# A home of their own for a pair's rows, statistics two tiles ahead, and a later wait for the low-rank operands in a fused attention and FFN kernel

## The reference, cut to what matters

```python
xn = _layernorm(x)                        # x: (4, 512, 1024), over the last axis
qkv = xn @ w_qkv                          # 32 query heads, 8 key and 8 value heads of 128
scores = einsum('bqhgd,bkhd->bhgqk', q, k) * scale
bias = -slope[h] * sqrt(max(pos_q - pos_k, 0)), -inf where pos_k > pos_q
attn = einsum(softmax(scores + bias), v) @ w_o
out = xn @ W.T + b                        # the FFN branch, 1024 x 1024
probs = softmax(xn @ gate_w.T + gate_b)   # 4 experts; one chosen, weight top / top
out += (xn @ A[:r].T @ B[:, :r].T) of the chosen rank r in (8, 16, 32, 64)
x + attn + out
```

## Time and profile before

| | us |
|---|---|
| median of three runs | 2610.23 (2610.15 to 2610.34) |
| the profiled execution's own time | 2612.52 |
| its span, first to last instruction | 2610.7 |
| PE busy | 2495.8 (96% of the span) |
| DVE busy | 1639.0 (63%) |
| ACT busy | 1026.0 (39%) |
| POOL busy | 174.7 (7%) |
| mean granted TensorE clock | 0.982 |

### The profile page before, as it was taken

How to read it: one execution, slowest core, us unless ns; L and a number is a source line. 1 busy time by engine, 2 the same in 40 slices (tenths; PEclk the granted TensorE clock), 3 DMA queues, 4 the chain that set the end, 5 groups by cost and what they waited for, 6 DMA issues and landing times.

```text
span 2610.7 us, 32277 instructions
## 1 busy us (share of the span) xinstructions
PE 2495.8 (96%) x12512; PEld 2129.1 (82%) x12512; DVE 1639.0 (63%) x3305; ACT 1026.0 (39%) x2123; POOL 174.7 (7%) x230
## 2 busy tenths in 40 slices
PE   4999899997799989999799999999999999999998
PEld 3788688886678868888688888888888888888887
DVE  5746534564655545545767776777767776777763
ACT  4533212333534311333444444444444444444441
POOL 2210100001220010000100000000000000000000
PEclk8999999998999989999899999999999999999999
DMA  4545534555245453544632232323344232322321
GB/s 143 167 131 190 186 133 141 193 201 192 85 140 185 168 187 113 193 177 162 246 105 99 96 117 93 105 82 121 121 162 148 95 113 97 106 100 95 114 72 65
DMA packets 86489, 355.09 MB, mean 136 GB/s; under 512 B 8873, under 2 KB 9017, under 8 KB 77376
## 3 DMA queue, kind: packets, MB, share of 16 engines
q1 hardware_dynamic: 49680, 216.65, 24.1%
q0 software_dynamic: 36656, 136.38, 14.8%
HBM read 235.02 MB, written 117.97 MB: 135 GB/s over the span
## 4 chain that ended last, share of the span: by engine, by line
PE 91%; DVE 4%; issue 2%; ACT 2%; DMA 1%; POOL 0%; SPq 0%; DVEq 0%; ACTq 0%; POOLq 0%
PE ps L512 28%; PE ps L514 28%; PE ps L513 28%; PE ps L699 5%; PE ps L595 1%; DVE stats L968 1%; ACT res_hi L753 0%; DMA rows_a<-x 0%; DVE w_lo L953 0%; DVE res_a L1044 0%; DVE res_a L953 0%; DVE res_b L953 0%; DVE res_b L1044 0%; DMA qk_s<-res_b 0%; ACT w_hi L753 0%
## 5 line engine op out<-in xcount | busy, mean ns | idle before, releaser
L953 DVE TENSOR_TENSOR w_lo<-raw,w_hi 128x1024 fp32r<-128x1024 f32 x196 | 238.9, 1223 | 374.0 <-ACT w_hi L753 373.9
L512 PE MATMUL ps<-x_hi,w_hi 128*128 128x512 f32 x1120 | 436.2, 389 | 0.0
L514 PE MATMUL ps<-x_hi,w_lo 128*128 128x512 f32 x1120 | 435.8, 389 | 0.0
L513 PE MATMUL ps<-x_lo,w_hi 128*128 128x512 f32 x1120 | 435.7, 389 | 0.0
L753 ACT ACTIVATE w_hi<-raw 128x1024 fp32r<-128x1024 f32 x196 | 207.0, 1059 | 580.6 <-PE ps L514 458.8
L512 PE MATMUL ps<-wo_hi,at_hi 128*128 128x512 f32 x1024 | 411.6, 402 | 1.4 <-DVE at_lo L953 1.4
L514 PE MATMUL ps<-wo_hi,at_lo 128*128 128x512 f32 x1024 | 400.6, 391 | 0.0
L513 PE MATMUL ps<-wo_lo,at_hi 128*128 128x512 f32 x1024 | 398.2, 389 | 0.0
L892 ACT ACTIVATE probs<-probs,neg_max 128x512 f32<-128x512 f32 (+3 forms) x512 | 283.6, 563 | 193.6 <-DVE neg_max L1189 193.6
L1222 DVE TENSOR_TENSOR acc<-ps,acc 128x512 f32<-128x512 f32 x256 | 176.6, 690 | 164.2 <-issue 135.4
L753 ACT ACTIVATE at_hi<-ps 128x512 fp32r<-128x512 f32 x128 | 76.7, 599 | 509.9 <-PE ps L514 509.9
(11 more groups left out here) (151 smaller groups left out, 4062.4 us busy)
## 6 DMA issues: line engine op xcount, KB each, us to landing
raw<-w_all SPq DMA_DIRECT2D x70, 1024.0 KB, 5.1
q<-qk_s SPq DMA_DIRECT2D x128, 512.0 KB, 3.8
qk_s<-res_hi POOLq DMA_DIRECT2D x40, 1024.0 KB, 4.6
wo_raw<-w_o SPq DMA_DIRECT2D x64, 512.0 KB, 4.3
qk_s<-res_a POOLq DMA_DIRECT2D x20, 1024.0 KB, 9.0
qk_s<-res_b POOLq DMA_DIRECT2D x20, 1024.0 KB, 5.3
k<-qk_s SPq DMA_DIRECT2D x32, 512.0 KB, 3.8
v<-v_s SPq DMA_DIRECT2D x32, 512.0 KB, 5.8
```

The costliest lines, as they stand in the source:

```text
L512: pe.matmul(to, st_hi, mv_hi, start=start, stop=False, skip_group_check=True)
L513: pe.matmul(to, st_hi, mv_lo, start=False, stop=False, skip_group_check=True)
L514: return pe.matmul(to, st_lo, mv_hi, start=False, stop=stop, skip_group_check=True)
L953: nc.vector.tensor_tensor(to, source, high.bitcast(F32), ALU.subtract).then_inc(signal, 1)
```

## The change

- The eight rows of a pair get a buffer `rows` of 32 KB at offset 16 KB, which is the place of `x_hi` slots 2 to 5; tile t lies over slot t + 2. SP loads tile t of the second pair once LAST's step t + 2 has ended, its last reader. `rows_a`, `rows_b` and their reuse go. At the start of the program SP issues the four rows of tiles 0 and 1, then the first weights, the four rows of tiles 2 and 3, and the other three weight blocks.
- Statistics, reciprocals and normalisation of a tile go together and run two tiles ahead: tile 1 at st 5 of LAST, tile 2 at st 6, tile 3 after copies of turn 1 and `second_tile(0)`. At the start of the program tile 1 stands before the first weights, tile 2 behind them.
- Turns 2 and 3 wait for `s_x0_lo` (the low part copied out of the bank) where they waited for `s_t1`, since the order of the DVE no longer implies it.
- FFN goes from fourth to sixth of the matrices, right before LAST.
- PE waits for `s_lora_in` and `s_u_lo` right before the first `lora` product of step 1.

```diff
-VALUES, KEYS, Q0, FFN, Q1, Q2, Q3 = range(MATRICES)
+VALUES, KEYS, Q0, Q1, Q2, FFN, Q3 = range(MATRICES)
...
-        rows_a = at("rows_a", 192 * K, [P, 3, HIDDEN])
-        rows_b = at("rows_b", 168 * K, [P, 2, HIDDEN])
+
+        rows = at("rows", 16 * K, [P, TT, HIDDEN])
...
+            def tokens(pr, t):
+
+                if pr:
+                    sp.wait_ge(s_bank, 4 * (number(pr - 1, LAST, t + 2) + 1))
+                for j in range(2):
+                    sp.dma_start(rows[:, 2 * t + j, :],
...
-                if m == FFN and st == 1:
-                    pe.wait_ge(s_u_lo, 3 * (pr + 1))
-                    pe.wait_ge(s_lora_in, 32 * (pr + 1))
...
                         if kt == KT - 1 and extra is not None:
+                            if st == 1 and s == 0:
+                                pe.wait_ge(s_u_lo, 3 * (pr + 1))
+                                pe.wait_ge(s_lora_in, 32 * (pr + 1))
                             last = lora(bank_of(n, s), s, *extra)
...
                     if t >= 2:
-                        pe.wait_ge(s_t1, pr * QT + t)
+                        pe.wait_ge(s_x0_lo, pr * QT + t)
...
                 for t in range(1, QT):
                     turned_tile(pr, t)
-                    if t + 1 < QT:
-                        deviation(pr, t + 1)
                     second_tile(pr, t - 1)
-                    if t + 1 < QT:
-                        normalised(pr, t + 1)
+                    if t + 2 < QT:
+                        deviation(pr, t + 2)
+                        normalised(pr, t + 2)
...
                     if st == 5:
                         deviation(pr + 1, 1)
+                        reciprocals(pr + 1, 1)
                     if st == 6:
                         turned_tile(pr + 1, 0)
-                        reciprocals(pr + 1, 1)
+                        deviation(pr + 1, 2)
+                        reciprocals(pr + 1, 2)
```

More of the change, by code:

```diff
@@ L134, in block_program @@
         s_const = sem("s_const")
-        s_rows = [sem(f"s_rows{i}") for i in range(5)]
+        s_rows = [sem(f"s_rows{i}") for i in range(TT)]
         s_raw = [sem(f"s_raw{i}") for i in range(4)]
@@ L260, in loaded @@
             return 16 * ((2 * g + 2) if st == 6 else (2 * g + 1) if WEIGHT[st] == 3 else g + 1)
[L264 to L268, removed]
         def turned(pr, t):
@@ L309, in _ @@
             sp.dma_start(ident[:, :], consts[:, SEQ:SEQ + P]).then_inc(s_ident, 16)
[L311 to L320, removed]
+            def tokens(pr, t):
[3 more added lines that the diff above has]
+                    sp.dma_start(rows[:, 2 * t + j, :],
+                                 x[bass.ds((pr * 2 + j) * SEQ + t * P, P), :]).then_inc(s_rows[2 * t + j], 16)
             def weights(pr, m, i, st):
@@ L330, in _ @@
             weights(0, 0, 0, None)
-            for i in range(2, 5):
-                tokens(0, i)
+            tokens(0, 2)
+            tokens(0, 3)
             for i in range(1, 4):
                 weights(0, 0, i, None)
-            for i in range(5, TT):
-                tokens(0, i)
             for pr in range(PAIRS):
@@ L351, in _ @@
                     sp.dma_start(raw[3][:, :], w_all[m, 3]).then_inc(s_raw[3], 16)
+                    if m == LAST and follow is not None:
+                        tokens(pr + 1, 0)
                     if follow is not None:
@@ L362, in _ @@
                         if m == LAST:
-                            for i in range(5, TT):
-                                tokens(pr + 1, i)
+                            tokens(pr + 1, 3)
             sp.wait_ge(s_bank, 4 * (number(PAIRS - 1, LAST, 2) + 1))
@@ L780, in normalised @@
                 for j in range(2):
-                    tile = row_tile(pr, 2 * t + j)[0]
+                    tile = rows[:, 2 * t + j, :]
                     nc.scalar.activation(tile, tile, ACT.Identity, bias=shift[:, 2 * t + j:2 * t + j + 1],
@@ L964, in deviation @@
                 for j in range(2):
-                    tile, landed = row_tile(pr, 2 * t + j)
-                    dve.wait_ge(*landed)
+                    dve.wait_ge(s_rows[2 * t + j], 16 * (pr + 1))
                     for half in range(2):
-                        last = nc.vector.bn_stats(stats[:, j, half, :], tile[:, half * 512:(half + 1) * 512])
+                        last = nc.vector.bn_stats(stats[:, j, half, :],
+                                                  rows[:, 2 * t + j, half * 512:(half + 1) * 512])
                 link(last)
```

39 lines of the change are left out of this document (21 added, 18 removed).

## The result

| | before | after |
|---|---|---|
| median of the runs on the same chip, us | 2610.19 (2608.99 to 2610.34) | 2571.05 (2568.85 to 2574.92) |
| profiled execution's time / span, us | 2612.52 / 2610.7 | 2568.85 / 2567.1 |
| PE busy | 2495.8 | 2485.7 |
| mean granted TensorE clock | 0.982 | 0.991 |

The ratio of the medians is 0.9853, with an interval of 0.9836 to 0.987. The time is 39.1 us less by the medians and 43.6 by the two profiled spans. The two differ because of the executions that were profiled: before, it lay 2.3 us above its median, and now it is the fastest of its four. In the runs further down the kernel before lies anywhere from 2608.2 to 2613.82 us, so two of its executions agree within 0.2%, not within a few hundredths. Two of its executions in the second group of experiments were slow runs (5045.9 and 5865.81 us) and are left out of all that follows.

The account below looks back on a forecast made before the run. PE's waits were taken to bound the kernel, at both first steps and in FFN. Gains of 8.1 + 9.3 + 23.0 = 40.4 us off 2610.2 gave 2569.8 us, range 2562 to 2580.

Parts of the forecast that it names:

- What bounds the kernel: PE's waits count in three places: both first steps, chains through DVE, ACT and PE, and FFN.
- Start of pair 0: At program start, turn 3 comes at 42.8 and step 1 at 53.7, 8.1 us earlier; bounds 5 and 14.
- Between the pairs: Turn 0 gains 3.5 us, turn 1 2.0, and step 1 comes 9.3 us earlier; bounds 2.0 and 14.
- FFN: Step 1's later wait for low-rank operands gains 11.2 and 11.8 us, together 23.0; ends 20 and 24.9.
- I charge no clock: In FFN's step 1, matmuls behind the remaining waits of 1.3 and 1.1 us run without a slow clock.
- Sum and median: Whole kernel: gains sum to 40.4 us, span 2570.3, median of runs 2569.8.
- Small DVE operations behind POOL: Rival, first steps: POOL's operations hold reciprocals, 1.0 us more each, up to 9 in all: 2577; chance 0.10.
- PE's pace: Rival: the loops run at PE's pace and both first steps gain 14 us: 2559; chance 0.07.
- Operands later: Rival in FFN: low-rank operands land 3 us later each: 2576; chance 0.06.
- nothing in the first steps: Rival: a wait as long takes its place in the first steps, only 23.0 gained: 2587; chance 0.05.
- The clock stays low: Rival: after first-step waits the clock stays at 1.2 GHz, 0.2 us more per matmul, some 2620 after 250; chance 0.04.
- FFN sixth costs nothing: Moving FFN to sixth, with rows at 16 KB, adds no instruction and was costed at nothing.

Follow-up runs that it names:

- old_order: Changed kernel with statistics back in their old order (one tile ahead, weights ahead of turn 0's copies), rows in the new buffer: 2577.63 us.
- adds_first: Changed kernel, but in LAST's step 6 of pair 0 DVE does step 5's adds before the next matrix's first low half: 2568.49 us.
- after_again: The changed kernel run again without edit, as base on the chip of a later group: 2577.26 us.
- copies_first: adds_first, with ACT also copying LAST's step 6 into `res_hi` before tile 2's square root and normalisation: 2565.6 us.
- start_too: copies_first, with tile 2's statistics at program start ahead of the first weights' low halves, its square root between their high halves: 2559.99 us.
- late_only: The kernel before with only the wait for the low-rank operands moved late: 2591.23 us.
- ffn_fourth: Changed kernel with FFN back in fourth place of the matrices: 2570.11 us.
- lora_last: Changed kernel with the four low-rank products of FFN's step 1 placed behind all its 48 matmuls: 2570.02 us.

## Why the prediction was right, point by point

- **What bounds the kernel.** The three places it named hold 42.1 of 43.6 us, and the sum agrees within 0.1 with the start of attention, so nothing else ahead of it moved by more. The other 1.5 lie in attention, where the clock over the first 40 us was 0.96 against 0.87.
- **Start of pair 0**: 8.1 forecast, 8.57 measured. Turns 1 to 3 came at 18.68, 32.21 and 42.33, forecast near 19, 32.3 and 42.8. Step 1 is 10.94 after turn 3, forecast 10.93. Tile 1's rows were there in time, as assumed. old_order shows the share of the order in it, 6.8.
- **Between the pairs**: 9.3 forecast, 9.16 measured. Turn 0 waits 6.70 (forecast 6.6), turn 1 follows 16.28 later (about 16) and turn 3 another 17.39 later (17). The reading that turn 0 would gain only 3.5, "because the reciprocals and normalisation now stand in front of the adds", is what adds_first undid, for 3.9 us.
- **FFN**: 23.0 forecast, 24.4 measured. Mechanism right, one term mis-sized: the waits left, 1.3 and 1.1, were 0.57 and 0.37 in this trace. I had kept the landing fixed to the issue, at 11.6 us; in the runs `lora_lo` takes between 9.4 and 11.4 us over nine traces with the late wait, which leave between nothing and 1.7 us to wait. In the trace of the changed kernel it takes 11.4 us in pair 0, where PE arrives 0.6 later after the issue than I had reckoned, and 10.4 in pair 1. The upper end, 24.9 "(all of it gone)", doesn't follow from its own terms: 12.45 + 12.88 is 25.3.
- **"I charge no clock"** behind those waits: right in the first execution, wrong in after_again, where it cost 4.8 us behind 1.53 of waiting. The row that I rested it on had 1.91 us of waiting and full clock behind it. One such row shows that it can go well, and no more. In the nine traces with the late wait, stalls up to 1.42 us (copies_first) had full clock behind them, and those of 1.53 and 1.72 had 24 and 7 slow matmuls. In the trace that counted the stalls were 0.57 and 0.37, shorter than the 1.3 and 1.1 that I had forecast; what the clock would have done behind those is not shown there.
- **Sum and median**: 40.4 against 43.6 by spans and 39.1 by medians. 2569.8 is 1.3 below the first median. That closeness is in part luck: the profiled executions put the scatter on the side of a larger gain, the medians on the other. Over its twelve executions in three groups of runs the median is 2572.5, and the highest, 2578.66, is still inside 2562 to 2580.
- **Small DVE operations behind POOL** (2577): it went the other way. The chain of reciprocals, all eight tiles together, in the kernel before and in the changed one (groups of instructions: busy us, mean ns):

```profile
L983 DVE SCALAR_TENSOR_TENSOR newton<-moments,rstd 128x2 f32<-128x2 f32 x8 | 2.6, 331 | 0.3
L984 DVE SCALAR_TENSOR_TENSOR newton<-newton,rstd 128x2 f32<-128x2 f32 x8 | 2.3, 289 | 0.3
```

```profile
L974 DVE SCALAR_TENSOR_TENSOR newton<-moments,rstd 128x2 f32<-128x2 f32 x8 | 1.3, 160 | 0.3
L975 DVE SCALAR_TENSOR_TENSOR newton<-newton,rstd 128x2 f32<-128x2 f32 x8 | 1.3, 161 | 0.3
```

Now none of them is held. What is held is an operation on two buffers of SBUF beside POOL, at the same place:

```profile
630.74 1.68 DVE L944 TENSOR_TENSOR x_lo<-x_raw,x_hi 128x512 fp32r<-128x512 f32 x1 [2.04 <-POOL x_raw L405]
...
650.30 0.69 DVE L944 TENSOR_TENSOR x_lo<-x_raw,x_hi 128x512 fp32r<-128x512 f32 x1 [2.69 <-POOL x_raw L405]
```

And POOL at the first of them:

```profile
630.59 1.28 POOL L399 TENSOR_TENSOR x_raw<-x_raw 128x512 f32<-128x512 f32 x1
```

The first of the two lies beside POOL's operation from 630.59 to 631.87 and takes 1.68 us. The second, which POOL's last operation of the stretch releases, takes 0.69. That is what the rule of the Trainium skill says ("SBUF — State Buffer", section "SBUF: two separate sides", an exclusive lock in which the loser blocks for the whole instruction). The trace agrees with it: the held operation ends 0.55 us after POOL's, having started 0.15 after it. What was wrong was to expect the hit on the reciprocals. The 0.9 us that the sum had for it between the pairs were spent all the same, on this operation (1.68 - 0.69 = 0.99); at the start of pair 0 0.40 of the 0.5 it had, where the same operation took 1.09 us.
- **PE's pace** (2559): not in this order, since ACT and DVE still work one behind the other. start_too takes some of that apart and, as another kernel, comes to 2559.99.
- **Operands later** (2576), **nothing in the first steps** (2587): neither; late_only, which is the second of them made on purpose, took 2591.23.
- **The clock stays low**: no. Step 1 of VALUES ran at full clock in both pairs (PEclk 1.00 over 53.27:64.70 and 652.34:663.80). It fell behind FFN's wait, for 24 matmuls in one trace of the changed kernel out of three.
- **FFN sixth costs nothing**: ffn_fourth shows no difference, within 0.2 us by the traces.

## What to carry to other kernels

When work is run further ahead on an engine that works in order, look at what it now stands in front of: here the same move that shortened three turns lengthened the wait of the first, and putting the adds and copies that PE waits for ahead of it was worth another 7 us. Put a wait on the instruction that reads the operand, not on the loop around it, and leave some slack behind its forecast landing, because a short stall can also cost the clock (4.8 us behind 1.53 here, though lora_last, which has the slack, can't be told from the changed kernel by its median). Before believing a difference of a few microseconds, run the same kernel again: three medians of one program lay 6 us apart.

## What the hardware showed unexpectedly

- A stall of 1.53 us was followed by 24 matmuls at 1.2 GHz (4.8 us) in one execution, and one of 1.72 us at the same place by seven (1.4 us, adds_first); stalls of 1.42, 1.24, 1.22 and 1.05 us were followed by none, nor, at another place, was one of 1.91. These runs don't tell what decides it.
- The clock behind the same 9.3 us stall in front of attention was granted at 0.96 or at 0.85 to 0.87 over 40 us, in executions of one program: 3 to 4 us of scatter in a part that the change doesn't touch.
- The low-rank operands (two transfers of 260 KB behind transfers of 1 MB) land at a time that varies: `lora_lo` took from 9.4 (after_again) to 11.6 us (the kernel before) from issue to landing. With the early wait PE stood 8.54 and 8.95 us in one kernel, 9.90 and 10.08 in another.
